# Deformable attention with a positional-bias MLP: row-tiled bias corrections shared between neighbouring steps

## What is computed

```python
pos = grid_q[:, :, None, :] - grid_kv[:, None, :, :]
bias = jnp.sign(pos) * jnp.log1p(jnp.abs(pos))
bias = jax.nn.relu(bias @ cpb_w1 + cpb_b1)        # 2 -> 32
bias = jax.nn.relu(bias @ cpb_w2 + cpb_b2)        # 32 -> 32
bias = (bias @ cpb_w3 + cpb_b3)                   # 32 -> 1
sim = jnp.einsum('bhid,bhjd->bhij', qh, kh) + bias
attn = jax.nn.softmax(sim, axis=-1)
out = jnp.einsum('bhij,bhjd->bhid', attn, vh)
```

## Time and profile before

| | |
|---|---|
| median of 3 runs | 914.47 us (913.43 to 914.48) |
| the profiled execution | 915.55 us, span 913.5 us |
| TensorE matmul busy | 848.0 us, 93% of the span |
| VectorE busy | 711.9 us, 78% |
| ScalarE busy | 657.2 us, 72% |
| GpSimd busy | 71.2 us, 8% |
| mean granted TensorE clock | 0.970 |

### The profile page before, as it was taken

The page is one execution under the profiler, slowest core; times in us unless marked ns, Lnnn a source line. Parts: engine busy times, 40 slices in busy tenths (PEclk is TensorE's granted clock), DMA queues, the critical chain, the costliest instruction groups (busy, mean ns, idle before and its releaser), DMA issues.

```text
span 913.5 us, 33809 instructions
## 1 busy us (share of the span) xinstructions
PE 848.0 (93%) x15524; PEld 290.2 (32%) x15524; DVE 711.9 (78%) x493; ACT 657.2 (72%) x773; POOL 71.2 (8%) x40
## 2 busy tenths in 40 slices
PE   2299999899999999899999999989999999999986
PEld 1133233333333333323333333323333333333322
DVE  4699698898877688899885878889887768888811
ACT  2368678867776687887776877886777768777761
POOL 2120003210000004040000001240000000000000
PEclk8589999999999999999999999999999999999998
DMA  3301001020020101002020101002020010200000
GB/s 148 89 20 40 13 2 52 7 53 5 9 58 14 50 3 50 8 3 56 3 64 14 49 4 33 20 8 54 5 57 20 8 46 2 74 3 3 3 15 35
DMA packets 23804, 27.44 MB, mean 30 GB/s; under 512 B 15600, under 2 KB 17520, under 8 KB 23664
## 3 DMA queue, kind: packets, MB, share of 16 engines
q1 hardware_dynamic: 23664, 25.29, 10.4%
HBM read 23.05 MB, written 2.10 MB: 28 GB/s over the span
## 4 chain that ended last, share of the span: by engine, by line
issue 56%; PE 30%; POOL 6%; DVE 3%; DMA 2%; ACT 2%; SPq 0%; ACTq 0%; POOLq 0%; DVEq 0%
PE pair L797 10%; PE scores L811 9%; PE pair L792 4%; POOL conv_prod L315 3%; POOL big L422 3%; PE pair L934 2%; DVE h L589 1%; PE pair L943 1%; PE scores L821 1%; PE pair L918 1%; DMA att_den<-reciprocals_dram 1%; PE pair L900 1%; ACT h L442 1%; PE scores L906 1%; PE pair L925 0%
## 5 line engine op out<-in xcount | busy, mean ns | idle before, releaser
L442 ACT ACTIVATE h<-pair 128x1024 f32<-128x1024 f32 x512 | 496.4, 1021 | 189.9 <-PE pair L797 184.5
L589 DVE TENSOR_TENSOR h<-hx,hy 128x2048 f32<-128x2048 f32 x256 | 581.3, 2301 | 37.7 <-PE pair L797 37.4
L797 PE MATMUL pair<-h,wts 32*32 32x512 f32 x8192 | 352.3, 601 | 6.9 <-DVE h L589 6.8
L811 PE MATMUL scores<-h,wts 128*32 128x512 f32 x2048 | 277.0, 613 | 0.1
L792 PE MATMUL pair<-fy,u_rows 32*32 32x512 bf16 x4096 | 127.4, 387 | 29.6 <-DMA fy<-fy_dram 16.8
L797 PEld LDWEIGHTS pair<-h,wts 32*32 32x32 f32 x8192 | 134.0, 103 | 26.7 <-DVE h L589 10.2
L811 PEld LDWEIGHTS scores<-h,wts 128*32 128x32 f32 x2048 | 40.6, 108 | 218.5 <-issue 216.0
L792 PEld LDWEIGHTS pair<-fy,u_rows 32*32 32x32 bf16 x4096 | 40.0, 88 | 200.4 <-issue 170.0
L315 POOL TENSOR_TENSOR conv_prod<-qpad,wts 128x288 f32<-128x288 f32 x16 | 31.3, 1985 | 425.6 <-ACT qpad L469 425.6
L422 POOL TENSOR_TENSOR big<-big,hat_x 128x512 f32<-128x512 f32 x16 | 37.2, 2350 | 119.1 <-DVE big L687 119.1
L716 DVE TENSOR_REDUCE neg_max<-pair 128x8 f32<-128x512 f32 x32 | 22.1, 690 | 29.7 <-PE pair L900 29.3
(11 more groups left out here) (89 smaller groups left out, 381.1 us busy)
## 6 DMA issues: line engine op xcount, KB each, us to landing
hx<-features_dram SPq DMA_DIRECT2D x64, 128.0 KB, 2.8
hy<-features_dram SPq DMA_DIRECT2D x64, 128.0 KB, 3.2
att_den<-reciprocals_dram SPq DMA_DIRECT2D x8, 256.0 KB
wts<-weights_dram SPq DMA_DIRECT2D x2, 960.0 KB, 7.7
x<-x_dram SPq DMA_DIRECT2D x2, 512.0 KB, 5.4
fy<-fy_dram SPq DMA_DIRECT2D x64, 6.0 KB
fy<-fy_dram SPq DMA_DIRECT2D x64, 4.0 KB
fy<-fy_dram SPq DMA_DIRECT2D x64, 2.0 KB
```

The lines of the kernel that those rows point to most:

```text
L442: emptied("z", 2 * g + j, act.activation(h2[g % H2_BUFS][:, 2 * j:2 * (j + 1)].rearrange("p r n -> p (r n)"), pair_of("z", 2 * g + j)[:], ...
L589: dve.tensor_tensor(h1[g % H1_BUFS][:].rearrange("p c (y x) -> p c y x", x=W), hx[unit % 2][:, :, t].unsqueeze(2).broadcast_to([128, CT, H ...
L797: ins = pe.matmul(z[r][32 * c:32 * (c + 1)], w(l, "w2")[key[r], key[r]], h1[g % H1_BUFS][key[r], c], start=False, stop=True)
L811: ins = pe.matmul(scores[phase % 2][32 * r:32 * (r + 1)], w(l, "w3")[:, 32 * t:32 * (t + 1)], h2[g % H2_BUFS][:, r], start=t == 0, stop=t ...
```

## The change

The corrections of a row for all four keys become one matmul of 32 rows by 128 columns, so four a step in place of 16. Those of rows 2 and 3 no longer begin their sum but end it, and are issued at the head of the next step, just ahead of those of rows 0 and 1 of that step. `h2` is split by halves, each with two buffers instead of three. `layer3` in step g takes rows 0 and 1 of step g-1 and rows 2 and 3 of step g-2. ScalarE does the relu of rows 2 and 3 of the step before, then that of rows 0 and 1. The first layer's buffer is given back by a semaphore of its own, `h1_used`. The slots of the softmax and of what hangs on it move by one step. `ring` and `RING` are as before.

```diff
-H1_BUFS = H2_BUFS = 3
+H1_BUFS = 3
+H2_BUFS = 2
 RING = 3
...
-SOFTMAX_SLOTS = {("pe", "scores_t"): 1, ("dve", "score_max"): 3, ("act", "widen_max"): 2,
-                 ("pe", "max_off"): 3, ("act", "exp"): 3}
+SOFTMAX_SLOTS = {("pe", "scores_t"): 2, ("dve", "score_max"): 4, ("act", "widen_max"): 3,
+                 ("pe", "max_off"): 4, ("act", "exp"): 4}
...
                 if g >= H2_BUFS:
-                    act.wait_ge(bias_added, g - H2_BUFS + 1)
...
+                    act.wait_ge(bias_added, g - H2_BUFS + 1 + j)
...
-                act.wait_ge(bias_added, STRIDES * (phase + 1))
+                act.wait_ge(bias_added, STRIDES * (phase + 1) + 1)
...
+                if 1 <= g <= ALL_STEPS:
+                    relu2(g - 1, 1)
                 if g < ALL_STEPS:
-                    for j in range(2):
-                        relu2(g, j)
-                if g and g % STRIDES == 0 and g <= ALL_STEPS:
+                    relu2(g, 0)
+                if g > STRIDES and g % STRIDES == 1 and g <= ALL_STEPS + 1:
                     copy_scores(g // STRIDES - 1)
...
                 if g >= H1_BUFS:
-                    wait_filled(dve, "z", 2 * (g - H1_BUFS) + 1)
+                    dve.wait_ge(h1_used, g - H1_BUFS + 1)
...
+            def correction(g, r, **flags):
+
+                unit, h, t = g // UNIT_STEPS, g // STRIDES % 2, g % STRIDES
+                y = fy[unit % 2][key_rows(r), t, H // 2 * h:H // 2 * (h + 1)]
+                return pe.matmul(z_of(g, r), u_rows[unit // PAIRS // B][key_rows(r)],
+                                 y.unsqueeze(2).broadcast_to([32, H // 2, W]), **flags)
+
+            def corrections(g):
+
+
+                if g:
+                    correction(g - 1, 2, start=False, stop=True)
+                    filled("z", 2 * (g - 1) + 1, correction(g - 1, 3, start=False, stop=True))
+                if g < ALL_STEPS:
+                    unit = g // UNIT_STEPS
+                    if g % UNIT_STEPS == 0:
+                        pe.wait_ge(fy_loaded[unit % 2], 16 * 3 * ROWS * (unit // 2 + 1))
+                        pe.wait_ge(u_ready, unit // PAIRS // B + 1)
+                    turn("z", 2 * g)
+                    correction(g, 0, start=True, stop=False)
+                    correction(g, 1, start=True, stop=False)
+
             def layer2(g):
...
+                turn("z", 2 * g + 1)
                 pe.wait_ge(h1_ready, g + 1)
                 for r in range(ROWS):
                     for c in range(CT):
...
+                        ins = pe.matmul(z_of(g, r)[32 * c:32 * (c + 1)], w(l, "w2")[key_rows(r), key_rows(r)],
+                                        h1[g % H1_BUFS][key_rows(r), c], start=r >= 2, stop=r < 2)
+                    if r == 1:
+                        filled("z", 2 * g, ins)
+                ins.then_inc(h1_used, 1)
...
+                for step, rows in ((g - 1, (0, 1)), (g - 2, (2, 3))):
+                    if not 0 <= step < ALL_STEPS:
+                        continue
...
+                    wait_emptied(pe, "z", 2 * step + rows[0] // 2)
...
+                if g <= ALL_STEPS:
+                    corrections(g)
                 if g < ALL_STEPS:
                     layer2(g)
-                if 1 <= g <= ALL_STEPS:
-                    layer3(g - 1)
+                if 1 <= g <= ALL_STEPS + 1:
+                    layer3(g)
```

More of the change, by code:

```diff
@@ L78 @@
     ("pe", "image_t", 0): 30, ("act", "image_t_out", 0): 30, ("dve", "conv_sum", 0): 33,
[L79 to L83, removed]
@@ L84 @@
-    ("pool", "hat_products", 0): 42, ("pool", "hat_products", 1): 44, ("dve", "hat_products", 0): 45,
-    ("dve", "hat_products", 1): 46, ("pe", "sample", 0): 47, ("dve", "sample_out", 0): 49,
-    ("pe", "keys_values", 0): 50, ("act", "keys_values_out", 0): 50,
+    ("dve", "conv_sum", 1): 34, ("act", "conv_gelu", 0): 33, ("pe", "offset", 0): 35,
+    ("act", "offset_tanh", 0): 35, ("dve", "positions", 0): 38, ("pe", "spread", 0): 37,
+    ("act", "features", 0): 37, ("act", "spread_out", 0): 38, ("dve", "features_sign", 0): 40,
@@ L87 @@
+    ("act", "distances", 0): 39, ("act", "distances", 1): 40, ("act", "distances", 2): 41,
+    ("act", "distances", 3): 42, ("dve", "hats", 0): 43, ("dve", "hats", 1): 45,
+    ("pool", "hat_products", 0): 43, ("pool", "hat_products", 1): 45, ("dve", "hat_products", 0): 46,
+    ("dve", "hat_products", 1): 47, ("pe", "sample", 0): 48, ("dve", "sample_out", 0): 50,
+    ("pe", "keys_values", 0): 51, ("act", "keys_values_out", 0): 51,
 }
 AFTER_SLOTS = {
-    ("pe", "attend", 0): 5, ("act", "attend_out", 0): 5, ("dve", "reciprocal", 0): 8, ("dve", "divide", 0): 11,
@@ L92 @@
-    ("pe", "project", 0): 11, ("dve", "residual1", 0): 13, ("pe", "mlp_up", 0): 13, ("act", "mlp_gelu", 0): 13,
-    ("pe", "mlp_up", 1): 14, ("act", "mlp_gelu", 1): 14, ("pe", "mlp_down", 0): 16, ("dve", "residual2", 0): 18,
-}
-SOFTMAX_SLOTS = {("pe", "scores_t"): 1, ("dve", "score_max"): 3, ("act", "widen_max"): 2,
-                 ("pe", "max_off"): 3, ("act", "exp"): 3}
+    ("pe", "attend", 0): 5, ("act", "attend_out", 0): 5, ("dve", "reciprocal", 0): 9, ("dve", "divide", 0): 12,
+    ("pe", "project", 0): 12, ("dve", "residual1", 0): 14, ("pe", "mlp_up", 0): 14, ("act", "mlp_gelu", 0): 14,
@@ L98 @@
+    ("pe", "mlp_up", 1): 15, ("act", "mlp_gelu", 1): 15, ("pe", "mlp_down", 0): 17, ("dve", "residual2", 0): 19,
+}
+SOFTMAX_SLOTS = {("pe", "scores_t"): 2, ("dve", "score_max"): 4, ("act", "widen_max"): 3,
+                 ("pe", "max_off"): 4, ("act", "exp"): 4}
 TERMS_SLOT = 12
@@ L223, in build @@
         h1 = [sb(f"h1_{k}", [128, CT, HALF]) for k in range(H1_BUFS)]
-        h2 = [sb(f"h2_{k}", [128, ROWS, HALF]) for k in range(H2_BUFS)]
+        h2 = [[sb(f"h2_{j}{k}", [128, ROWS // 2, HALF]) for k in range(H2_BUFS)] for j in range(2)]
         w1y_of_key = sb("w1y_of_key", [128, 128])
@@ L267, in build @@
         h1_ready = sem("h1_ready")
+        h1_used = sem("h1_used")
         bias_added = sem("bias_added")
@@ L440, in relu2 @@
                 if g >= H2_BUFS:
-                    act.wait_ge(bias_added, g - H2_BUFS + 1)
-                emptied("z", 2 * g + j, act.activation(h2[g % H2_BUFS][:, 2 * j:2 * (j + 1)].rearrange("p r n -> p (r n)"),
+                    act.wait_ge(bias_added, g - H2_BUFS + 1 + j)
+                emptied("z", 2 * g + j, act.activation(h2[j][g % H2_BUFS][:].rearrange("p r n -> p (r n)"),
                                                        pair_of("z", 2 * g + j)[:], ACT.Relu))
@@ L776, in _, with key_rows, z_of @@
         def _(pe):
-            def layer2(g):
[L780 to L793, removed]
+            def key_rows(r):
+                return slice(32 * r, 32 * (r + 1))
+            def z_of(g, r):
+                return pair_of("z", 2 * g + r // 2)[:, bank(r % 2)]
+            def correction(g, r, **flags):
[15 more added lines that the diff above has]
+                    correction(g, 1, start=True, stop=False)
+            def layer2(g):
+                l = g // UNIT_STEPS // PAIRS // B
+                turn("z", 2 * g + 1)
                 pe.wait_ge(h1_ready, g + 1)
@@ L796, in layer2 @@
                     for c in range(CT):
[L797 to L800, removed]
-            def layer3(g):
[L804 to L812, removed]
+                        ins = pe.matmul(z_of(g, r)[32 * c:32 * (c + 1)], w(l, "w2")[key_rows(r), key_rows(r)],
[3 more added lines that the diff above has]
+                ins.then_inc(h1_used, 1)
+            def layer3(g):
+                for step, rows in ((g - 1, (0, 1)), (g - 2, (2, 3))):
+                    if not 0 <= step < ALL_STEPS:
+                        continue
+                    phase, t = step // STRIDES, step % STRIDES
+                    l = step // (SEG_STEPS * B)
+                    if t == 0 and phase >= 2:
+                        pe.wait_ge(exp_ready, phase - 1)
+                    wait_emptied(pe, "z", 2 * step + rows[0] // 2)
+                    for r in rows:
+                        ins = pe.matmul(scores[phase % 2][32 * r:32 * (r + 1)], w(l, "w3")[:, 32 * t:32 * (t + 1)],
+                                        h2[rows[0] // 2][step % H2_BUFS][:, r % 2], start=t == 0, stop=t == STRIDES - 1,
+                                        skip_group_check=True)
                 ins.then_inc(bias_added, 1)
```

## The result

The changed kernel takes 1012.29 us (1011.22 to 1015.11, 4 runs) against 914.44 us: ratio 1.108, 95% interval 1.105 to 1.111. The forecast was 1038 us, in a range of 985 to 1080. The span of the profiled execution went from 913.5 to 1009.2 us, by 95.7 us.

A forecast was written before the change was run, and what follows sets the result against it. The prediction took TensorE, busy 93% of the span, to set the pace. Its terms, -7 + 96 + 21.5 + 7 + 22 - 15.5 = +124 us on 915.55, gave 1039.5, as a median 1038 us; range 985 to 1080.

The forecast's parts named there:

- The new wait: Behind a ring stage, layer 2 waits for corrections, then relu of rows 2 and 3: +1.16 us in 83 steps, +96 us.
- Stages ahead of the relu: ScalarE's part of a step's stages now precedes the relu of its rows 2 and 3, lengthening the wait: +21.5 us.
- The exp with its table load: In plain steps, exp and table load precede that relu and delay the following layer 2: +7 us (0 to 13).
- The wide correction: In 172 plain steps, faster layer 2 against form change and longer load: -0.04 us each, -7 us (-33 to +33).
- the prediction's other estimate: Plain steps by TensorE's 64-instruction queue rule: about 0.09 us a step gained net, 15 us in place of 7.
- The rival in which the change of form is not paid back: Plain steps: layer 2 gains nothing, form change and load add 0.15 us each, +26 us, so 1071 us; chance 0.10.
- the one in which the wide corrections do not run beside each other: Corrections' weight loads follow each other, 0.25 us longer in each of 255 steps: about 1100 us; chance 0.05.
- The partly hidden wait: ScalarE's part is short in most steps, no clock falls, the queue gain is whole: about 967 us; chance 0.09.
- The clock: TensorE falls to half of 2.4 GHz behind new long waits, 1.58 us a fall: +22 us (0 to 46).
- I take half of these: Of 29 steps with TensorE idle 1.7 to 2.1 us, half lose the clock: 14 x 1.58 = +22 us.
- What goes away: Old delays of layer 3 vanish: 7.5 us behind 31 `scores_t` steps, 8 us in nine VectorE waits; -15.5 us.
- The faster rival: At the `turn` ahead of layer 2 the pair is free, each of 255 steps gains 0.1 us: 889 us; chance 0.03.

The follow-up runs named there:

- e2: The changed kernel, but a single stage between two steps takes the pair of rows 0 and 1 of its step (spread, u_rows excepted): 957.38 us, ratio 1.047.
- e5: The changed kernel, but ScalarE does its part of a step's stages behind the relu of that step's rows 2 and 3, not ahead: 999.66 us, ratio 1.097.
- e3: The changed kernel with the skew kept, but 16 corrections of 32x32 a step as before: 1020.04 us, ratio 1.116.
- e1: The kernel before with only the four wide corrections in place of 16, at their old place, no skew, old slots: 924.0 us, ratio 1.009.
- e8: The changed kernel, skewed only in the 172 steps no ring stage follows, with three buffers for each half of h2: 905.78 us, ratio 0.993.
- e9: e1, but the relu of rows 0 and 1 works on row 0 alone and layer 3 reads zeros for row 1: 885.91 us, ratio 0.969.

## Why the prediction was right

The time lies in the range because the mechanism is the forecast one. The rise is 98 us where 124 were forecast, and the 26 us between them are errors of single terms, named below.

**The new wait** was the mechanism, as forecast, and e2 shows it by changing the pair alone. The two buffers of `h2`, costed at nothing, were not tested apart; no relu of the changed kernel waits for `layer3` in its list of waits. Its length: the relu starts 0.44 us after the corrections (0.50 forecast), layer 2 at 1.51 us (1.58), layer 3 at 2.60 us (2.66). In 83 steps that makes (2.60 - 1.50) x 83 = 91 us, forecast 96. Most of the 0.06 us a step is the start of the relu, which was put too late.

**Stages ahead of the relu** measured in the starts of layer 2: `mlp_up` 2.34 us (2.35 forecast); `attend` 2.19 (2.20 forecast); `q` and `image_t` 2.10 (2.11); `keys_values` 2.52 (2.48); `project` 1.76 (1.78). What I missed is `spread`, at 2.26 us, where the features with their table load come ahead. Against 1.51 us these add up to 26 us; 21.5 were forecast. Also missed are three of the `scores_t` steps, at 2.40 us behind `distances`: 2.7 us more. e5 takes nearly all of this wait away, but the time falls by only 12.6 us: in this kernel the term is worth about half of what the waits add up to. The waits for VectorE and for `work` grow in e5, as its list shows; why they do was not tested.

The exp with its table load was put at 7 us and cost about 2. The forecast let the load start 0.27 us into the step and layer 2 of the step after be 1.37 us late. In the changed kernel the load starts 0.45 us ahead of the step, and layer 2 comes 0.99 us behind the corrections where 0.32 is plain, so it is 0.67 us late:

```profile
87.30 1.28 ACT L538 ACT_TABLE_LOAD   x1
87.75 0.39 PE L790 MATMUL pair<-fy,u_rows 32*128 32x512 bf16 x4
...
90.17 0.47 PE L790 MATMUL pair<-fy,u_rows 32*128 32x512 bf16 x4
91.16 1.15 PE L816 MATMUL pair<-h,wts 32*32 32x512 f32 x32 [0.52 <-ACT h L444]
```

There are seven such plain steps. Before there were four, each with layer 3 about 0.65 us late. The difference is 2 us.

**The wide correction** in a plain step gives 0.07 us, in 172 steps 12 us (forecast 0.04 us, 7 us; the prediction's other estimate, 0.09 us a step, has 15 us). Both halves of the sum are visible in e3: 0.07 to 0.09 us more between corrections and layer 2, where change of form and load together were put at 0.15 (0.11 + 0.04), and 0.17 us back in layer 2 (0.19). No run separates the form from the load. The load's own record is only 3 ns longer, 91 ns against 88 ns for 32 columns before, so most of the 0.04 us was too much. The rival in which the change of form is not paid back falls by e3, the one in which the wide corrections do not run beside each other by their records: four in 0.40 us. The partly hidden wait, 967 us, falls by the 125.3 us that TensorE does wait and by the five more falls of the clock.

**The clock** is the term that was most mis-sized, and it is 14 of the 26 us between forecast and result. I took 14 more falls of 1.58 us, 22 us. Within the steps the trace has four stretches at half of 2.4 GHz before and nine after, each 3.4 us long: five more, about 8 us. (That is one execution: its mean granted clock is 0.968, that of the three others 0.965 to 0.966.) Of the 29 steps with the long waits only four had such a fall, one behind `keys_values` and three behind `attend`, and none of the twelve behind `mlp_up`; the other five falls came in steps behind `scores_t`. The windows of the changed kernel show a wait that had no such effect, the one of 1.94 us behind `mlp_up` above (first two rows, the wait and what follows), and a stretch that did fall, at 404.80 us:

```profile
290.80:293.10 2.30, 0.40 (x5) 0.10 (x4) 0.00 (x0) 2.18 (x3) 0.00 (x0) 1.00 0.05 7
293.10:298.00 4.90, 4.86 (x52) 1.35 (x54) 2.29 (x1) 1.02 (x1) 0.00 (x0) 1.00 0.16 57
404.80:408.20 3.40, 3.14 (x40) 0.49 (x40) 2.67 (x2) 1.29 (x3) 0.00 (x0) 0.50 0.00 0
```

Around the start of the stretch that fell TensorE waited 0.99 and 0.85 us, neither of them long by itself:

```profile
403.00 0.63 PE L924 MATMUL pair<-const,probs 128*128 128x128 f32 x4 [0.99 <-ACT h L444]
403.56 0.65 PE L790 MATMUL pair<-fy,u_rows 32*128 32x512 bf16 x4
...
405.06 2.02 PE L816 MATMUL pair<-h,wts 32*32 32x512 f32 x32 [0.85 <-ACT h L444]
```

So a length of wait read off two waits of the kernel before does not tell which waits cost the clock. The step that failed is "I take half of these". The rest of the 26 us: 5 from the plain step, 5 from the chain's shorter length, 5 from the exp, less 7 for the stages that cost more than forecast. That makes 22; the remainder is among small terms. What goes away was sized about right: the forecast has 15.5 us, and the trace before has 9.3 us behind `scores_t` and 8.3 us in the nine steps that waited for VectorE.

**The faster rival** named the right place, the `turn` ahead of layer 2. Its price, 0.1 us a step in 255 steps, was too simple. e1 frees rows 2 and 3 of the chain and is slower than before, since the pair then comes free 0.13 us too late. With the relu at its full length the gain of the wide corrections needs the skew, and e8 has both.

## What to carry to other kernels

Skewing work by a step moves the point at which a buffer is full; before doing it, list for every distance in the ring of buffers who holds that buffer next and whether its release now lies behind the work that waits for it. Here the skew was right in the 172 steps whose next user was another, and cost 1.1 us and more in the 83 where it was the same. A step that is shortened by 0.07 us or more gains that only if the chains beside it have the slack: before, the relu of rows 0 and 1 ended at 2.42 us of a 2.49 us step, so there were just 0.07 us.

## What was not expected of the hardware

- A bf16 weight load of 32 rows by 128 columns is hardly longer in the records than one of 32x32, 91 against 88 ns. Of float32 loads with 128 rows, those of 128 columns took 140 to 260 ns by group and those of 32 columns 108 to 110.
- Layer 2 is slower with more instructions straight ahead of it: 1.27 us to layer 3 behind 32 (e3), 1.10 behind 8 in the changed kernel and 1.07 behind 8 in e1 and e9, 1.08 behind a wait, with the same matmuls. The Trainium skill, "TensorE: Matmul & The Clock Gate" (table at its head), gives a queue of 64 instructions, and layer 2 alone has 64; that 32 ahead cost more than 8 agrees with it, but no run here shows the queue.
- A wait of 1.94 us left TensorE's clock at its full 2.4 GHz, and two shorter ones close together, of 0.99 and 0.85 us, went with 3.4 us at 1.2 GHz.
